# Three attention heads' bias bands added by TensorE in three 16-bit parts instead of two 32-bit parts

## The chip, the cores and the metric

The kernel runs on one core of a Trainium2 chip. The metric is the device time of one execution in microseconds (us); before, the median of three runs is 2453.97 us (2453.03 to 2454.3). One more execution was taken with the hardware profiler; all rows below come from it.

## What is computed

The program is a chain of six residual layers over x, four sequences of 1024 rows with 256 features: a mixture of experts, an attention, the mixture again, a quantized linear layer, a second attention of 16 heads, and the linear layer again. The change lies in the second attention:

```python
q = proj(Wq) / math.sqrt(DH)      # DH = 16, 16 heads
k = proj(Wk)
v = proj(Wv)
scores = jnp.einsum('bhid,bhjd->bhij', q, k)
i = jnp.arange(T)
dist = jnp.clip(i[:, None] - i[None, :], 0, MAX_REL)   # MAX_REL = 128
bias = rel[:, dist]
scores = scores + bias[None]
causal = i[:, None] >= i[None, :]
scores = jnp.where(causal[None, None], scores, -jnp.inf)
attn = jax.nn.softmax(scores, axis=-1)
y = jnp.einsum('bhij,bhjd->bhid', attn, v)
```

The bias of a head depends on the distance alone and is the same beyond 128, so after the far value is taken off it is zero everywhere but in a band of 256 columns beside the diagonal. The causal mask is put into the same band.

## The kernel before, in words

Two stages matter. The linear layer in front of the second attention (`linear`) carries other work in its gaps, step by step. `HeadTables` splits the attention's weights and builds the bands; `HeadProjection` normalizes, transposes and projects the first sequence. `beside_steps` sets their order: 28 steps of the tables come first, then each step of the projection, and beside every second one a further step of the tables. Each engine runs its own part of this list in order.

The tables are built for eight pairs of heads (`hp`). SP fetches a pair's band from a scratch tensor, TensorE (PE) flips it, ScalarE (ACT) copies it to `full` (L1672), and PE transposes it for the maxima (`flip_turn`). In step `part 0` ACT copies `full` into the first part of `band` (L1680), rounded to the 32-bit matmul format, and for every second pair one head's band to `band_dve` (L1679). In step `part 1` GpSimd (POOL) subtracts the first part from `full` and writes the second part (L1659), and ACT copies the transposed band to `band_q`. A pair's copy to `full` waits for the POOL subtraction of the pair before. POOL's queue also holds the gathers of the linear layer's input (L1379), whose sums VectorE (DVE) makes.

The heads' stage (`attention_heads`) then works on 16 units, each four heads (`HG`) of one sequence. A unit has 12 cells of key block (128 keys) and half of the queries (up to 512), and each cell has four scores, one for each head. PE multiplies a score (L2273) into one of three banks. In nine of the 12 cells the band meets the cell. There PE adds the band for the first three heads (`HP`): two matmuls of a 32-bit identity `ident_r` by the parts of `band` (L2277), with 256 columns in six cells and 128 in three. For the fourth head DVE adds `band_dve` in the bank (L2208). ACT takes the exponential (L2133), and PE multiplies it by the values (L2294). PE may start score n+1 only when the exponential of score n-2 is done.

Between the scores PE, in an order written out by `heads_order`, computes the scores of later units a first time (L2253) into three other banks. DVE takes their row maxima (L2170, L2179 and, with `band_q` added, L2182). In the first two units of a sequence the projection of the next one stands in the same lists.

## Time and profile before

| | before |
|---|---|
| median of the runs | 2453.97 us |
| the profiled execution | 2455.88 us |
| its span in the trace | 2453.8 us |
| PE busy | 2067.1 us (84%) |
| DVE busy | 1482.1 us (60%) |
| ACT busy | 955.9 us (39%) |
| POOL busy | 308.8 us (13%) |

The time of the profiled execution is its span and some 2 us around it. Matmuls overlap, and their ends are modelled: a matmul's duration is longer than its distance from the next one, so costs of PE are read from start to start. The chain of waits is followed back from the last instruction and says which engine's work set the end of the program; busy shares alone do not.

### The profile page before, as it was taken

What the parts mean: (1) busy time and instruction counts of PE and PEld (TensorE: products, weight loads), DVE (VectorE), ACT (ScalarE), POOL (GpSimd) and SP (SyncE); (2) the same over time, 40 slices, a digit from 0 to 9 for tenths busy, and PEclk for the clock granted to TensorE, in tenths of its full rate; (3) what the DMA queues carried; (4) which work ended last, traced back from release to release, by engine and by line L of the source; (5) the groups of instructions that cost most, each with busy time, mean ns of one, the idle gap of its engine ahead of it and who ended that gap; (6) DMA issues with size and microseconds to landing.
All of it is one profiled execution on the core that took longest, in us unless ns stands there. A gap on an engine that the chain in (4) does not pass through costs nothing.

```text
span 2453.8 us, 38491 instructions
## 1 busy us (share of the span) xinstructions
PE 2067.1 (84%) x12810; PEld 1556.0 (63%) x12810; DVE 1482.1 (60%) x4378; ACT 955.9 (39%) x1944; POOL 308.8 (13%) x300
## 2 busy tenths in 40 slices
PE   5689999966999975899999836578998998999966
PEld 3578888855878854788888725424554455545445
DVE  7844444446555578444444388677786686687548
ACT  4222232322333343223233234325555555655643
POOL 4420000022000033300000062311001101100000
PEclk8799999987999987999999967769999999999988
DMA  8111010111000022201010130342242242333002
GB/s 270 54 58 30 27 31 27 32 52 41 1 1 1 1 69 79 84 21 32 27 31 27 33 112 15 77 54 60 41 53 53 54 53 47 59 43 39 3 9 69
DMA packets 84043, 114.83 MB, mean 47 GB/s; under 512 B 12216, under 2 KB 73824, under 8 KB 80736
## 3 DMA queue, kind: packets, MB, share of 16 engines
q1 hardware_dynamic: 77424, 94.80, 17.5%
q0 software_dynamic: 6432, 17.57, 2.2%
q8 instruction: 113, 1.85, 0.3%
q14 instruction: 74, 0.61, 0.1%
HBM read 69.17 MB, written 43.17 MB: 46 GB/s over the span
## 4 chain that ended last, share of the span: by engine, by line
PE 61%; DVE 26%; ACT 4%; issue 4%; DMA 2%; POOL 2%; SPq 0%; DVEq 0%; ACTq 0%; POOLq 0%
PE psum L775 10%; PE psum L777 10%; PE psum L776 10%; PE psum L2294 4%; PE psum L126 4%; PE psum L128 4%; PE psum L127 4%; DVE mt L2182 4%; PE psum L2273 3%; PE psum L862 3%; DVE m L2170 3%; DVE m L2179 2%; PE psum L2253 2%; DVE stats L160 2%; PE psum L2277 2%
## 5 line engine op out<-in xcount | busy, mean ns | idle before, releaser
L2133 ACT ACTIVATE pt<-psum 128x512 f32<-128x512 f32 (+3 forms) x768 | 334.0, 492 | 273.0 <-DVE psum L2208 180.2
L740 DVE SCALAR_TENSOR_TENSOR h<-psum,xg,sg 128x128 f32<-128x128 f32 x592 | 166.6, 344 | 415.6 <-PE psum L862 415.6
L556 ACT ACTIVATE sg<-psum 128x512 f32<-128x512 f32 x180 | 107.7, 598 | 544.2 <-PE psum L777 544.2
L775 PE MATMUL psum<-w_hi,xt_hi 128*128 (+1 forms) x720 | 286.2, 398 | 17.9 <-DVE xt_lo L705 17.3
L776 PE MATMUL psum<-w_lo,xt_hi 128*128 (+1 forms) x720 | 284.2, 395 | 0.0
L777 PE MATMUL psum<-w_hi,xt_lo 128*128 (+1 forms) x720 | 283.7, 394 | 0.0
L2253 PE MATMUL psum<-ks,qs 96*128 96x512 bf16 (+3 forms) x768 | 234.8, 346 | 43.0 <-DMA ks<-qk_scr 18.8
L2273 PE MATMUL psum<-qs,ks 99*128 99x512 bf16 (+3 forms) x768 | 238.3, 333 | 24.7 <-ACT pt L2133 19.1
L775 PE MATMUL psum<-w_hi,ht_hi 128*128 (+1 forms) x720 | 217.1, 302 | 0.3
L2277 PE MATMUL psum<-band,ident_r 128*128 128x256 f32 (+1 forms) x864 | 215.0, 337 | 0.0
L2182 DVE CUSTOM_DVE_ANT_0 mt<-psum,band_q 128x256 bf16<-128x256 f32 (+1 forms) x512 | 204.2, 399 | 17.1 <-PE psum L2253 6.9
L777 PE MATMUL psum<-w_hi,ht_lo 128*128 (+1 forms) x720 | 203.2, 282 | 0.0
L776 PE MATMUL psum<-w_lo,ht_hi 128*128 (+1 forms) x720 | 201.9, 280 | 0.0
L2273 PEld LDWEIGHTS psum<-qs,ks 99*128 99x128 bf16 x768 | 68.8, 98 | 188.4 <-ACT pt L2133 112.3
L2170 DVE TENSOR_REDUCE m<-psum 128x1 f32<-128x512 f32 (+1 forms) x256 | 166.9, 652 | 34.0 <-PE psum L2253 30.4
L775 PEld LDWEIGHTS psum<-w_hi,xt_hi 128*128 128x128 f32 x720 | 137.0, 190 | 43.4 <-issue 19.4
L2277 PEld LDWEIGHTS psum<-band,ident_r 128*128 128x128 f32 x864 | 149.9, 194 | 19.0 <-issue 0.3
L2294 PE MATMUL psum<-pt,v 128*17 128x512 f32 (+3 forms) x1536 | 161.6, 494 | 0.0
L777 PEld LDWEIGHTS psum<-w_hi,xt_lo 128*128 128x128 f32 x720 | 136.8, 190 | 30.0
L776 PEld LDWEIGHTS psum<-w_lo,xt_hi 128*128 128x128 f32 x720 | 137.2, 190 | 22.6
L2253 PEld LDWEIGHTS psum<-ks,qs 96*128 96x128 bf16 x768 | 68.9, 99 | 117.6 <-DVE m L2182 45.7
L776 PEld LDWEIGHTS psum<-w_lo,ht_hi 128*128 128x128 f32 x720 | 136.4, 189 | 0.0
(283 smaller groups left out, 4248.6 us busy)
## 6 DMA issues: line engine op xcount, KB each, us to landing
xg<-w_dram SPq DMA_DIRECT2D x54, 256.0 KB, 3.2
qk_scr<-parts SPq DMA_DIRECT2D x32, 384.0 KB, 2.5
qs<-qk_scr SPq DMA_DIRECT2D x96, 128.0 KB, 7.0
ks<-qk_scr SPq DMA_DIRECT2D x96, 128.0 KB, 7.7
xg<-rows_in SPq DMA_DIRECT2D x74, 132.0 KB, 2.1
rows_out<-yb SPq DMA_DIRECT2D x74, 128.0 KB, 1.7
x<-x_dram SPq DMA_DIRECT2D x4, 1024.0 KB, 8.7
out_dram<-x SPq DMA_DIRECT2D x4, 1024.0 KB, 4.5
```

Of the source, the lines that this page charges most:

```text
L556: act.activation(sg[i % 2][:, :, :], up_banks(i)[:, :, 0:F], ACT.Silu).then_inc(*silu.up())
L740: ins = dve.scalar_tensor_tensor(out=h[i % 2][:, e, :], in0=u[:, e, :], scalar=xg[j % XSLOT][:, at:at + 1], in1=sg[i % 2][:, e, :], op0=AL ...
L775: pe.matmul(out, a[0], b[0], start=first, stop=False)
L776: pe.matmul(out, a[0], b[1], start=False, stop=False)
L777: return pe.matmul(out, a[1], b[0], start=False, stop=last)
L2133: act.activation(pt[n % NPT][:, 0:q1 - q0], st_bank(n)[:, 0:q1 - q0], ACT.Exp).then_inc(*exped.up())
L2170: dve.tensor_reduce(m3[u % 2][:, h * BT + t, 0:1], mx_ring.bank((kind, i))[:, 0:cut], AXIS.X, ALU.max).then_inc(*far_max.up())
L2182: dve.tensor_tensor_reduce(junk[:, 0:bw], bank[:, far - cut:w - cut], band_q[:, u % NHG * HG + h, 2 * P - bw:2 * P], 1.0, LOWEST, ALU.add, ...
L2253: pe.matmul(bank[:, 0:c1 - c0], qs[r][0:KS_ROWS, h, t * P:(t + 1) * P], ks[r][0:KS_ROWS, h, c0:c1], start=True, stop=True).then_inc(*(far_ ...
L2273: ins = pe.matmul(bank[:, 0:q1 - q0], ks[r][:, h, j * P:(j + 1) * P], qs[r][:, h, q0:q1], start=True, stop=not by_pe)
L2277: ins = pe.matmul(bank[:, 0:b1 - q0], tables.ident_r[:, :], band[:, part, u % NHG, h, q0 - j * P:b1 - j * P], start=False, stop=(part == 1))
L2294: ins = pe.matmul(y_banks[c][h * MQ:h * MQ + DH + 1, q0 - c * BANK:BANK], v1[b % 2][:, j, g * HG + h, :], slot[:, 0:(c + 1) * BANK - q0], ...
```

## The change

The bands of the three heads that PE adds are kept in three 16-bit parts instead of two 32-bit ones, and the identity that they are multiplied by is 16-bit too. So a band is three matmuls on PE instead of two. DVE adds the fourth head's band as before; the rewritten index and wait of that addition come to the same for one such head.

To make three parts, ACT writes the first part in 16 bits, POOL subtracts it from `full` into a new buffer `rest`, ACT writes the second part from `rest`, and POOL subtracts that from `rest` into the third part. This adds a step `part 2` for each pair, eight steps in all. The next pair's copy to `full` now waits for POOL's first subtraction (`rest_ok`), and POOL's first subtraction waits for the second one of the pair before (`left_ok`).

```diff
+        BPARTS = 3
...
-                self.ident_r = sb(stack, "ident_r", [P, P], F32R)
-                self.band = sb(stack, "band", [P, 2, NHG, HP, 2 * P], F32R)
-                self.band_dve = sb(stack, "band_dve", [P, NHG, 2 * P])
+                self.ident_b = sb(stack, "ident_b", [P, P], BF16)
+                self.band = sb(stack, "band", [P, BPARTS, NHG, HP, 2 * P], BF16)
+                self.band_dve = sb(stack, "band_dve", [P, NHG, HG - HP, 2 * P])
...
                     yield [("part", (hp, 1))]
+                    yield [("part", (hp, 2))]
...
-                elif kind == "part" and i[1] == 1:
+                elif kind == "part" and i[1] > 0:
                     hp, part = i
                     g, h0, n = self.heads_of(hp)
-                    pool.wait_ge(*self.part_ok(hp + 1))
-                    pool.tensor_tensor(self.band[:, 1, g, h0:h0 + n, :], self.full[:, 0:n, :],
-                                       self.band[:, 0, g, h0:h0 + n, :].bitcast(F32),
-                                       ALU.subtract).then_inc(*self.left_ok.up())
+                    near = lambda m: self.band[:, m, g, h0:h0 + n, :]
+                    if part == 1:
+                        if hp:
+                            pool.wait_ge(*self.left_ok(hp))
+                        pool.wait_ge(*self.part_ok(hp + 1))
+                        pool.tensor_tensor(self.rest[:, 0:n, :], self.full[:, 0:n, :], near(0),
+                                           ALU.subtract).then_inc(*self.rest_ok.up())
+                    else:
+                        pool.wait_ge(*self.mid_ok(hp + 1))
+                        pool.tensor_tensor(near(2), self.rest[:, 0:n, :], near(1),
+                                           ALU.subtract).then_inc(*self.left_ok.up())
...
                     if i:
-                        act.wait_ge(*self.left_ok(i))
+                        act.wait_ge(*self.rest_ok(i))
...
+                    if part == 2:
+                        act.wait_ge(*self.rest_ok(hp + 1))
+                        act.activation(self.band[:, 1, g, h0:h0 + n, :], self.rest[:, 0:n, :],
+                                       ACT.Copy).then_inc(*self.mid_ok.up())
...
-                                for part in range(2):
-                                    ins = pe.matmul(bank[:, 0:b1 - q0], tables.ident_r[:, :],
+                                for part in range(BPARTS):
+                                    ins = pe.matmul(bank[:, 0:b1 - q0], tables.ident_b[:, :],
                                                     band[:, part, u % NHG, h, q0 - j * P:b1 - j * P],
-                                                    start=False, stop=(part == 1))
+                                                    start=False, stop=(part == BPARTS - 1))
```

On PE the first cell of the first unit stood as follows before (`qs`, `ks`: the stacked queries and keys; L2273 a score, L2277 its band, L2253 a score for the maxima):

```order
L2273 MATMUL psum<-qs_133,ks_134 128x512
L2253 MATMUL psum<-ks_182,qs_181 128x512 x2
L2273 MATMUL psum<-qs_133,ks_134 128x512
L2277 MATMUL psum<-band,ident_r 128x256 x2
L2253 MATMUL psum<-ks_182,qs_181 128x128
L2273 MATMUL psum<-qs_133,ks_134 128x512
L2277 MATMUL psum<-band,ident_r 128x256 x2
```

And there it stands so now (lines are some 15 further down: L2288 a score, L2292 its band, L2268 a score for the maxima):

```order
L2288 MATMUL psum<-qs_133,ks_134 128x512
L2268 MATMUL psum<-ks_183,qs_182 128x512 x2
L2288 MATMUL psum<-qs_133,ks_134 128x512
L2292 MATMUL psum<-band,ident_b 128x256 x3
L2268 MATMUL psum<-ks_183,qs_182 128x128
L2288 MATMUL psum<-qs_133,ks_134 128x512
L2292 MATMUL psum<-band,ident_b 128x256 x3
```

Each band has a third matmul, and nothing else moved here.

On ACT the second half of the first sequence's projection stood so before, in the linear stage (`xn` the normalized rows, `xt_hi` and `rest` their transposed parts, `parts` the projected queries and keys, L1419 the linear layer's own):

```order
L1808 ACTIVATE xn<-xn,rstd_10 128x256 x4
L1817 ACTIVATE xt_hi<-psum,gamma_beta 128x512
L1819 ACTIVATE rest_131<-psum,gamma_beta 128x512
L1817 ACTIVATE xt_hi<-psum,gamma_beta 128x512
L1819 ACTIVATE rest_132<-psum,gamma_beta 128x512
L1828 ACTIVATE parts<-psum 128x512
L1831 ACTIVATE parts<-rest_131 128x512
L1419 ACTIVATE xt_hi<-psum 128x512 x2
```

And so now, with the last pair's steps among them:

```order
L1683 ACTIVATE band_full<-psum 128x512
L1823 ACTIVATE xn<-xn,rstd_10 128x256 x4
L1832 ACTIVATE xt_hi<-psum,gamma_beta 128x512
L1834 ACTIVATE rest_131<-psum,gamma_beta 128x512
L1690 ACTIVATE band_dve<-band_full 128x256
L1691 ACTIVATE band<-band_full 128x256
L1832 ACTIVATE xt_hi<-psum,gamma_beta 128x512
L1834 ACTIVATE rest_132<-psum,gamma_beta 128x512
L1843 ACTIVATE parts<-psum 128x512
L1846 ACTIVATE parts<-rest_131 128x512
L1699 ACTIVATE band_q<-psum 128x512
L1419 ACTIVATE xt_hi<-psum 128x512 x2
```

The copies of the last pair, which came before the projection, now stand inside it.

On POOL the same stretch read so before (`x` the residual rows, `xt_lo` and `parts` the projection's remainders):

```order
L1786 TENSOR_TENSOR x<-x,xn 128x1024
L1790 TENSOR_TENSOR xt_lo<-rest_131,xt_hi 128x512
L1790 TENSOR_TENSOR xt_lo<-rest_132,xt_hi 128x512
L1795 TENSOR_TENSOR parts<-rest_131,parts 128x512
L1795 TENSOR_TENSOR parts<-rest_132,parts 128x512
L1795 TENSOR_TENSOR parts<-rest_131,parts 128x512
L1795 TENSOR_TENSOR parts<-rest_132,parts 128x512
```

And so now:

```order
L1667 TENSOR_TENSOR band_rest<-band_full,band 128x512
L1671 TENSOR_TENSOR band<-band_rest,band 128x512
L1801 TENSOR_TENSOR x<-x,xn 128x1024
L1805 TENSOR_TENSOR xt_lo<-rest_131,xt_hi 128x512
L1805 TENSOR_TENSOR xt_lo<-rest_132,xt_hi 128x512
L1810 TENSOR_TENSOR parts<-rest_131,parts 128x512
L1667 TENSOR_TENSOR band_rest<-band_full,band 128x256
L1810 TENSOR_TENSOR parts<-rest_132,parts 128x512
L1810 TENSOR_TENSOR parts<-rest_131,parts 128x512
L1671 TENSOR_TENSOR band<-band_rest,band 128x256
L1810 TENSOR_TENSOR parts<-rest_132,parts 128x512
```

The two subtractions of each of the last two pairs now stand ahead of the projection's second half and within it.

## Rows read from the trace of the kernel before

**Rows 1.** The page, its first part: busy time, share and instructions of each engine.
```profile
PE 2067.1 (84%) x12810; PEld 1556.0 (63%) x12810; DVE 1482.1 (60%) x4378; ACT 955.9 (39%) x1944; POOL 308.8 (13%) x300
```

**Rows 2.** Windows of the heads' stage: length, each engine's busy us, clock, DMA.
```profile
1740.00:1780.00 40.00, 38.50 (x276) 19.35 (x276) 33.66 (x130) 23.07 (x53) 0.18 (x1) 1.00 0.33 42
...
2300.00:2340.00 40.00, 36.39 (x268) 17.96 (x265) 9.83 (x34) 26.59 (x62) 0.00 (x0) 1.00 0.01 2
```

**Rows 3.** The chain of waits from 1631 to 2357 us, shares by line.
```profile
by line: PE psum L2294 14.7%; DVE mt L2182 10.8%; PE psum L2273 10.7%; DVE m L2170 7.9%; issue 7.0%; PE psum L2253 6.4%; DVE m L2179 5.8%; PE psum L2277 5.1%; PE psum L126 3.3%; DVE psum L2208 3.1%; ACT pt L2133 2.8%; PE psum L128 2.4%; PE 
```

**Rows 4.** Grouped instructions, 1631 to 2357 us: busy us, mean ns, idle us before.
```profile
L2277 PE MATMUL psum<-band,ident_r 128*128 128x256 f32 x576 | 150.7, 350 | 0.0
L2277 PEld LDWEIGHTS psum<-band,ident_r 128*128 128x128 f32 x864 | 149.9, 194 | 19.0 <-issue 0.3
...
L2273 PEld LDWEIGHTS psum<-qs,ks 99*128 99x128 bf16 x766 | 68.6, 98 | 182.4 <-ACT pt L2133 112.3 <-issue 50.0
L2277 PE MATMUL psum<-band,ident_r 128*128 128x128 f32 x288 | 64.4, 311 | 0.0
...
L2273 PE MATMUL psum<-qs,ks 99*128 99x256 bf16 x128 | 32.2, 280 | 11.9 <-ACT pt L2133 11.9
...
L2273 PE MATMUL psum<-qs,ks 99*128 99x128 bf16 x128 | 28.4, 226 | 0.5 <-ACT pt L2133 0.4
```

**Rows 5.** Time line of PE, bands of 256 columns: start us, us, engine, line.
```profile
1756.98 0.38 PE L2273 MATMUL psum<-qs,ks 99*128 99x512 bf16 x1
1757.01 0.58 PE L2277 MATMUL psum<-band,ident_r 128*128 128x256 f32 x2
1757.45 0.39 PE L2273 MATMUL psum<-qs,ks 99*128 99x512 bf16 x1
```

**Rows 6.** Time line of PE, 16-bit matmuls of 256 and 512 columns.
```profile
1908.73 0.28 PE L2253 MATMUL psum<-ks,qs 96*128 96x256 bf16 x1
1908.84 0.38 PE L2273 MATMUL psum<-qs,ks 99*128 99x512 bf16 x1
1909.06 0.57 PE L2253 MATMUL psum<-ks,qs 96*128 96x512 bf16 x2
```

**Rows 7.** Time line of PE, bands of 128 columns behind scores of 512 and 128.
```profile
1777.24 0.38 PE L2273 MATMUL psum<-qs,ks 99*128 99x512 bf16 x1
...
1777.64 0.45 PE L2253 MATMUL psum<-ks,qs 96*128 96x384 bf16 x2
...
1779.49 0.22 PE L2273 MATMUL psum<-qs,ks 99*128 99x128 bf16 x1
...
1779.78 0.23 PE L2253 MATMUL psum<-ks,qs 96*128 96x128 bf16 x1
```

**Rows 8.** Time line of PE, a 16-bit matmul of 128 columns.
```profile
1773.11 0.22 PE L2253 MATMUL psum<-ks,qs 96*128 96x128 bf16 x1
1773.17 0.27 PE L2273 MATMUL psum<-qs,ks 99*128 99x256 bf16 x1
```

**Rows 9.** The chain's first and last band: start us, us, what.
```profile
1666.07 0.23 PE psum L2277 x2
...
2353.06 0.23 PE psum L2277 x2
```

**Rows 10.** Waits from 1631 to 2357 us: us in total, times, longest us.
```profile
ACT pt L2133 <- DVE psum L2208: 180.2, 113, 37.1
...
PEld psum L2273 <- ACT pt L2133: 112.3, 178, 3.4
```

**Rows 11.** The making of `band` (duration ns min/median/max), and one wait of ACT.
```profile
L1680 ACT ACTIVATE band<-band_full x8: 399/507/633, 1433.9 to 1505.8; 128x512 fp32r<-128x512 f32 x4, 128x256 fp32r<-128x256 f32 x4
L1659 POOL TENSOR_TENSOR band<-band_full,band x8: 730/1274/1705, 1441.0 to 1513.7; 128x512 fp32r<-128x512 f32 x4, 128x256 fp32r<-128x256 f32 x4
...
1449.57 0.60 ACT L1672 ACTIVATE band_full<-psum 128x512 f32<-128x512 f32 x1 [3.80 <-POOL band L1659]
```

**Rows 12.** The projection: a piece of the chain, and POOL's time line.
```profile
1558.76 0.68 ACT rest L1819
...
1568.68 1.17 POOL L1795 TENSOR_TENSOR parts<-rest,parts 128x512 bf16<-128x512 f32 x1 [2.43 <-ACT parts L1831]
```

More of the change, by code:

```diff
@@ L1561, in __init__ @@
                 self.flipped, self.fulled, self.flip_turned = S("flipped"), S("full"), S("flip_turned")
-                self.part_ok, self.left_ok, self.band_q_ok = S("band_part"), S("band_left"), S("band_q")
+                self.part_ok, self.rest_ok, self.mid_ok, self.left_ok, self.band_q_ok = (S(x) for x in (
+                    "band_part", "band_rest", "band_mid", "band_left", "band_q"))
             def allocate(self, stack):
@@ L1568, in allocate @@
                 self.stage = [sb(stack, f"table_stage{i}", [P, KD * D]) for i in range(2)]
-                self.full = sb(stack, "band_full", [P, 2, 2 * P])
+                self.full, self.rest = (sb(stack, s, [P, 2, 2 * P]) for s in ("band_full", "band_rest"))
             def order(self):
@@ L1635, in on_pool @@
                 if kind == "setup":
-                    pool.tensor_copy(self.ident_r[:, :], ident[:, :])
+                    pool.tensor_copy(self.ident_b[:, :], ident[:, :])
                     pool.memset(line[:, :], MASKED).then_inc(*self.line0.up())
@@ L1678, in on_act @@
                         if n < 2:
-                            act.activation(self.band_dve[:, g, :], self.full[:, n, :], ACT.Copy)
+                            act.activation(self.band_dve[:, g, h0 + n - HP:h0 + 2 - HP, :], self.full[:, n:2, :], ACT.Copy)
                         act.activation(self.band[:, 0, g, h0:h0 + n, :], self.full[:, 0:n, :],
                                        ACT.Copy).then_inc(*self.part_ok.up())
+                    if part == 2:
+                        act.wait_ge(*self.rest_ok(hp + 1))
+                        act.activation(self.band[:, 1, g, h0:h0 + n, :], self.rest[:, 0:n, :],
+                                       ACT.Copy).then_inc(*self.mid_ok.up())
                     if part == 1:
@@ L2129, in on_act @@
                             if near_of[cell] and h >= HP:
-                                act.wait_ge(*biased(u * len(near_cells) + near_cells.index(cell) + 1))
+                                act.wait_ge(*biased((u * len(near_cells) + near_cells.index(cell)) * (HG - HP) + HG - h))
                             else:
```

2 lines of the change are left out of this document (1 added, 1 removed).

## Prediction, made before the changed kernel ran

> **What bounds the kernel now.** I read the page first, then the grouped instructions of the stage that the change touches, then its chain of waits, and last single matmuls on the time line, because a mean duration does not tell how far apart pipelined matmuls run. The page [rows 1] shows TensorE (PE) busy for 84% of the span. The heads' stage lies between 1631 and 2357 us. Its windows [rows 2] show PE busy for 38.5 of 40 us and VectorE (DVE) for 33.7 in the middle of the stage, and at its end PE for 36.4 and DVE only for 9.8. So PE and DVE are both nearly full, and neither has the stage alone. The chain of waits says the same: band matmuls (L2277) hold 5.1% of these 726 us, or 37 us, while DVE's maxima (L2182, L2170 and L2179) hold 24.5% [rows 3]. The reader is to see two things. PE is busy, but only part of what its band matmuls do lies on the path. And the matmuls' mean durations (350 and 311 ns, against 280 and 226 ns of the 16-bit ones of the same widths [rows 4]) are no price: they overlap.
>
> **What one band costs on PE before.** On the time line [rows 5] the score matmul at 1756.98 us (512 columns, then a band of 256 columns in two parts) is followed by the next score at 1757.45, after 0.47 us. A 16-bit matmul of 512 columns without a band takes 0.22 us from start to start (1908.84 to 1909.06 [rows 6]). So two 32-bit parts of 256 columns take 0.25 us, 0.125 each. For 128 columns there are two cases [rows 7]: behind a score of 512 columns it is 1777.24 to 1777.64, 0.40 less 0.22, so 0.18; behind one of 128 columns it is 1779.49 to 1779.78, 0.29 less the score's own 0.06, so 0.23.
>
> **What one band will cost.** A 16-bit part is a matmul of the same kind as the score's. With 256 columns such a one takes 0.11 us from start to start (1908.73 to 1908.84 [rows 6]), and with 128 columns 0.06 (1773.11 to 1773.17 [rows 8]). The mean durations of the two widths differ by 54 ns [rows 4], the time of 128 columns; with that I take 0.109 and 0.057 inside the two roundings. Three parts are then 0.327 us for 256 columns and 0.171 for 128. The change gives TensorE half as many matmuls again, and a 16-bit one is hardly cheaper than a 32-bit one where 256 columns set the pace: +0.077 us. With 128 columns it saves 0.01 (behind 512) or 0.06 (behind 128).
> Counted over the stage: 576 matmuls of 256 columns are 288 bands, 288 of 128 columns are 144 [rows 4]; of these 48 stand behind a score of 512 columns (block 3 against the second query half) and 96 behind one of 128. That is 288 x 0.077 = +22.2 us, 48 x 0.01 and 96 x 0.06 = -6.2 us, in all **+16 us of TensorE's time**.
>
> The 16-bit identity must also be loaded more often, 1296 times instead of 864. A load lasts 194 ns for the 32-bit identity and 98 ns for 16-bit weights [rows 4], but the spacing of 0.06 us at 1773.11 [rows 8] holds for a matmul whose successor loaded weights of its own, so a 16-bit load fits under 128 columns. I put the loads at nothing; their cover is the matmul ahead. The Trainium skill, page "TensorE: Matmul & The Clock Gate", section "LDWEIGHTS (loading the stationary operand)", speaks against this: it gives a load the columns divided by 1.2 in ns, an estimated 107 ns for 128 columns, by which three parts of 128 columns would take 0.32 us and TensorE's total would be about +37 us. The trace's 0.06 us disagrees with that.
>
> **How much of it lies on the path.** The lower end comes from the chain: a path that exists can only become as long as its pieces. Between its first band piece (1666.07 us) and its last (2353.06) the chain holds 123 bands of 256 columns, 0.23 to 0.24 us each, and 39 of 128, 20 of them near 0.17 and 19 near 0.23 [rows 9]. Priced as above, 123 x 0.077 - 20 x 0.01 - 19 x 0.06 = +8 us. The upper end is the whole +16: PE sets the pace throughout. PE idles 112.3 us in 178 waits for ScalarE's exponentials before a score, and ScalarE idles 180.2 us for the sums that DVE makes of the fourth head [rows 10]; such waits swallow part of a later PE. I take **+10**, near the chain's end, since the windows show DVE close behind PE in the middle of the stage; only at its end, where DVE is busy for 9.8 of 40 us [rows 2], is PE alone. A chain read back from semaphores can also overstate PE, so the bound for a reading in which DVE paces is lower than +8: the share of L2277 in the chain, 37 us of the 103 us that bands take by the prices above, times +16 is +6, and I let it fall to +2.
>
> **Making the third part.** The tables' stage gains eight conversions on ScalarE (ACT) and eight subtractions on GpSimd (POOL), and its steps stretch by eight. The existing ones last 0.40 to 0.63 us on ACT and 0.73 to 1.71 us on POOL [rows 11]. Those of six pairs lie before about 1518 us, where the two engines have holes: ACT waited 3.8 us for the same POOL subtraction at 1449.57 [rows 11]. There the new waits (ACT's second part for POOL's remainder, POOL's third part for ACT) take the place of the wait on the old second part; POOL's gathers are queued behind, and DVE's combines wait for these, but the new wait is one of the old length. I take 0. The last pairs of heads (6 and 7) now fall into the projection, where the chain runs through ACT, POOL and PE in turn. There pair 7's two copies stand between the two halves of the turned input: the second half's last step (0.68 us at 1558.76) is on the chain [rows 12], and the copies ahead of it add about 0.3 + 0.4 us, below their 0.40 us each since ACT's instructions overlap. The rest of pairs 6 and 7 meets holes such as POOL's 2.43 us at 1568.68 [rows 12]. On SP the pairs' fetches stand ahead of the projection's stores as they did; that costs nothing. I take **+1** for this stage, 0 to +4; the upper end is that half of the eight subtractions, at 0.73 to 1.28, stand on the path.
>
> **Sum.** +10 +1 = +11 us. The profiled execution took 2455.88 us (2453.8 of span, 2.1 around it), so it would be 2466.9; the median of the runs stands 1.9 lower, at 2453.97, and gives **2465.0**. Some 0.2% (4.9 us) is what a measurement here can tell from no change.
>
> **Rivals.**
> 1. DVE paces the stage and PE's extra work falls into its waits. For it: the 24.5% of the chain in DVE's maxima [rows 3] and the 112.3 us of waits [rows 10]. Against it: PE at 38.5 of 40 us [rows 2]. It gives +2 to +4, about 2457.
> 2. PE paces the stage throughout. For it: the same 38.5 of 40 us. Against it: the DVE pieces of the chain. All of +16 plus 1 to 4 gives 2471 to 2474.
> 3. Faster: the loads of the 32-bit identity, not columns, space the bands everywhere. Then two loads of 194 ns give way to three of 98 [rows 4], -0.094 us for each of 432 bands, -41 us, of which the chain's share (37 of 103) is -15: 2439. It decides if a band of 256 columns costs as much as its two loads, 0.39 us; it costs 0.25 [rows 5].
> 4. The 16-bit loads do not hide behind each other when three stand in a row. Then a 128-column band costs 3 x 0.098 = 0.294: 48 x 0.114 + 96 x 0.064 = +11.6 instead of -6.2, +34 in all; at 10/16 on the path, +21 and +1: 2476. Against it: the 0.06 at 1773.11 [rows 8]. The Trainium skill's rule on loads, named above, is this rival's.
> 5. The third part comes at a price of its own: the projection's chain takes up each of the new steps of pairs 6 and 7, +4, beside the +10: 2468. Nothing in PE's prices changes; this is inside the range.
>
> **How the numbers follow.** Forecast (+6 to +14, the fifth with it) 0.56, the first 0.18, the second 0.16, the third 0.04, the fourth 0.06. The first lies mostly within 4.9 us; a little of the forecast may too. So faster 0.04, same 0.18, slower 0.78. The range runs from +2 (2456) to the second's upper end (2473), which leaves out the third, the fourth and the edge of the first.
>
> **What would show it.** In the profile after, the band matmuls' line has 1296 matmuls, with loads near 98 ns; in the time line a score of 512 columns with a band of 256 is 0.54 to 0.55 us from the next, and one of 128 columns 0.39; the chain's share of the band line grows from 5.1% to about 7%; the heads' stage is about 10 us longer, and its start moves by about 1 us. The forecast is wrong if three parts of 256 columns take 0.25 us or less, if the stage's length stays as it is while PE's waits for ACT (112.3 us [rows 10]) shrink by what the bands gained, or if the start of the heads moves by several us.

## The result, and the profile after

The changed kernel is slower. Timed beside the kernel before, its median was 2467.03 us against 2456.49, 10.5 us more; the ratio is 1.0037 with a 95% interval of [1.0023, 1.0052], or +9.1 us. In a second set it was 2463.22 against 2455.48, 7.7 us more; the ratio is 1.0032 [1.0019, 1.0044], or +7.9 us. The prediction was +11 us, 2465.0 on the base of 2453.97, with a range of +2 to +19. The total held, but two of its terms were wrong in opposite directions.

The profiled execution after took 2462.59 us, 6.7 more than the one before (2455.88). Cut at three instructions that stand in both kernels (POOL's copy of the identity, the first score and the band of the last score), the two spans compare so:

| us | before | after | difference |
|---|---|---|---|
| start to the tables' first step | 1409.60 | 1409.56 | 0.0 |
| tables and projection, to the first score | 220.42 | 223.52 | +3.1 |
| heads' stage, first to last score | 723.04 | 729.40 | +6.4 |
| after the last score | 100.76 | 98.32 | -2.4 |

The last line is no effect of the change: over the 14 profiles of this study this stretch took 98.1 to 100.8 us, in no order that follows what was edited. So two stretches hold the price: +6.4 where +10 was predicted, and +3.1 where +1 was.

First the page after, the line that answers to [rows 1]. PE has 432 matmuls more and is hardly busier by this line, PEld is less busy, and POOL has its eight subtractions:

```profile
PE 2071.6 (84%) x13242; PEld 1528.2 (62%) x13242; DVE 1486.7 (60%) x4378; ACT 964.0 (39%) x1952; POOL 317.3 (13%) x308
```

The grouped instructions of the heads' stage after, which answer to [rows 4] (busy us, mean ns, idle us before; L2292 is the band's line now):

```profile
L2292 PE MATMUL psum<-band,ident_b 128*128 128x256 bf16 x864 | 141.6, 273 | 0.0
...
L2292 PEld LDWEIGHTS psum<-band,ident_b 128*128 128x128 bf16 x1293 | 117.1, 98 | 45.8 <-issue 1.6
...
L2292 PE MATMUL psum<-band,ident_b 128*128 128x128 bf16 x429 | 46.8, 219 | 0.0
```

By busy time a band has become cheaper (141.6 + 46.8 us against 150.7 + 64.4), which is the trap of these columns: matmuls overlap. The time line of PE shows the price, from start to start (L2288 a score, L2268 a score for the maxima):

```profile
1760.56 0.38 PE L2288 MATMUL psum<-qs,ks 99*128 99x512 bf16 x1
1760.77 0.49 PE L2292 MATMUL psum<-band,ident_b 128*128 128x256 bf16 x3
1761.10 0.38 PE L2288 MATMUL psum<-qs,ks 99*128 99x512 bf16 x1
...
1781.11 0.38 PE L2288 MATMUL psum<-qs,ks 99*128 99x512 bf16 x1
1781.33 0.33 PE L2292 MATMUL psum<-band,ident_b 128*128 128x128 bf16 x3
1781.50 0.44 PE L2268 MATMUL psum<-ks,qs 96*128 96x384 bf16 x2
...
1783.36 0.22 PE L2288 MATMUL psum<-qs,ks 99*128 99x128 bf16 x1
1783.42 0.33 PE L2292 MATMUL psum<-band,ident_b 128*128 128x128 bf16 x3
1783.59 0.22 PE L2268 MATMUL psum<-ks,qs 96*128 96x128 bf16 x1
```

A score of 512 columns and its band of 256 now take 0.54 us instead of 0.47 [rows 5]; the medians over such cells from the third unit on are 0.547 and 0.467. A score of 512 with a band of 128 takes 0.39 instead of 0.40, and one of 128 with its band 0.23 instead of 0.29 [rows 7]. These are the prediction's prices to the hundredth. With the rounded 0.07 for a band of 256 instead of 0.077, the prediction's +16 us of PE's work becomes +14 (288 x 0.07 - 6.2); the expectations of the experiments below speak of that.

The chain of waits over the heads' stage after, by line, answers to [rows 3]. The band's share went from 5.1% to 8.1%, and the share of DVE's maxima (L2197, L2185, L2194) from 24.5% to 17.6%: PE has taken over part of a path that the two engines share.

```profile
by line: PE psum L2309 15.2%; PE psum L2288 12.2%; PE psum L2268 8.8%; PE psum L2292 8.1%; DVE mt L2197 7.7%; issue 6.3%; DVE m L2185 5.4%; DVE m L2194 4.5%; PE psum L126 3.3%; ACT pt L2148 3.1%; DVE psum L2223 2.9%; PE psum L2337 2.3%; PE 
```

**The stage cut into its 16 units.** The +6.4 us becomes plain when windows run from one unit's first score to the next one's. Four units before, as windows (length, busy us of PE, PEld, DVE, ACT and POOL, then PE's granted clock and last two figures of DMA): the sixth, ninth and tenth, which carry the projection of a later sequence, and the twelfth, which does not.

```profile
1880.18:1937.20 57.02, 51.50 (x340) 30.11 (x336) 38.18 (x128) 32.76 (x72) 10.93 (x10) 0.97 0.34 67
...
2011.72:2072.83 61.11, 53.24 (x339) 30.91 (x335) 41.32 (x145) 31.61 (x67) 8.47 (x7) 1.00 0.27 46
2072.83:2128.56 55.73, 50.14 (x339) 29.04 (x335) 38.20 (x129) 32.76 (x72) 10.93 (x10) 1.00 0.36 70
...
2165.68:2202.84 37.16, 35.71 (x260) 18.22 (x256) 30.45 (x117) 21.76 (x50) 0.18 (x1) 1.00 0.36 45
```

The same units after:

```profile
1884.77:1941.03 56.26, 50.98 (x367) 27.80 (x363) 38.35 (x129) 33.01 (x72) 10.92 (x10) 1.00 0.34 68
...
2016.76:2077.97 61.21, 54.20 (x366) 29.58 (x363) 41.21 (x144) 31.96 (x67) 8.48 (x7) 1.00 0.26 45
2077.97:2134.23 56.26, 50.98 (x367) 27.80 (x363) 38.36 (x129) 33.08 (x72) 10.92 (x10) 1.00 0.34 67
...
2172.03:2209.83 37.80, 36.77 (x287) 17.03 (x283) 30.46 (x117) 22.23 (x50) 0.18 (x1) 1.00 0.33 43
```

The twelfth unit grew by 0.64 us, and the seven units like it (third, fourth, seventh, eighth, eleventh, twelfth and fourteenth; "plain" below) by 0.62 on average, all of them at full clock. By the prediction's prices PE has 1.0 us more to do in each unit (+16 us over 16). The tenth, with the projection, grew by 0.53, and the ninth by 0.10 only. The sixth seems to have become shorter, from 57.02 to 56.26. Its clock column tells why: PE was granted 0.97 there before, on average between its two levels of 1.2 and 2.4 GHz, and 1.00 after. The dip lies between 1910 and 1920 us (0.83 there); from 1900 to 1910 us PE was busy for 8.36 us, just as in the same place of its twin, the tenth, which kept 1.00. The twin took 55.73 us, so the clock cost the kernel before 1.3 us in the sixth unit. With that unit at full clock the stage would have grown by 6.4 + 1.3 = 7.7 us, just under the +8 that the prediction read from the chain as the floor. The first unit was at 0.94 in both and is no measure: it took 62.33 us before and 62.03 after, and 62.3 in the two other profiles of kernels with three parts that are named further down (after_again and one_step).

The last two units are the prediction's "only at its end ... is PE alone". They grew hardly more than the plain ones, by 0.65 and 0.67 us, although DVE has little to do in them. The sixteenth, before and after:

```profile
2322.86:2353.06 30.20, 27.22 (x202) 13.71 (x198) 4.85 (x13) 20.82 (x49) 0.00 (x0) 1.00 0.00 1
```
```profile
2331.61:2362.48 30.87, 28.54 (x229) 12.41 (x225) 4.86 (x13) 20.93 (x49) 0.00 (x0) 1.00 0.01 1
```

What took up the rest there is shown by the runs without the fourth head's addition, below.

**Where the tables' +3.1 us arise.** The chain of waits in the first sequence's projection before (start us, us, what: L185 normalizes, L1871 turns the rows, L1790 and L1828 make the parts):

```profile
1547.14 1.29 DVE xn L185 x4
...
1556.09 0.45 PE psum L1871 x4
...
1559.51 1.27 POOL xt_lo L1790
...
1562.95 0.61 ACT parts L1828
```

And after:

```profile
1547.51 2.14 DVE xn L185 x4
...
1557.04 0.45 PE psum L1886 x4
...
1558.93 0.41 ACT band_dve L1690
1559.34 0.30 ACT band L1691
...
1561.06 1.26 POOL xt_lo L1805
```

The time lines of POOL and ACT after add two rows, and the line of the normalization gives its durations (ns, min/median/max):

```profile
1547.22 1.30 POOL L1671 TENSOR_TENSOR band<-band_rest,band 128x512 bf16<-128x512 f32 x1 [3.32 <-ACT band L1695]
```
```profile
1565.46 0.60 ACT L1843 ACTIVATE parts<-psum 128x512 bf16<-128x512 f32 x1 [4.48 <-PE psum L128]
```
```profile
L185 DVE TENSOR_SCALAR xn<-x,mean_var,rstd x4: 398/400/1249, 1547.4 to 1549.2; 128x256 f32<-128x256 f32 x4
```

Four pieces follow one another. The stretch starts 0.37 us later (1547.14 to 1547.51). DVE's normalization takes 2.14 us instead of 1.29, because one of its four instructions lasted 1249 ns instead of some 400: they began at 1547.4, while POOL was at the third part of pair 6 (1547.22 to 1548.52). The two copies of pair 7 stand on the chain with 0.41 + 0.30 us, as the prediction had them, and the start of L1805 is 1.55 us late by then. Last, PE's part of the projection up to ACT's L1843 takes 4.40 us (1561.06 to 1565.46) instead of 3.44, at a granted clock of 0.50, the lower level of 1.2 GHz throughout, against 0.78 in the windows of these matmuls (1562.45 to 1565.50 after, 1560.91 to 1562.95 before). Together that is +2.5 us at 1565.46, and +3.1 at the first score; the last 0.6 us were not taken apart.

This sum of pieces is one profile's, and the stretch is not the same length in every profile of the same tables. With the maxima as they are it took 220.4 and 220.6 us in two profiles with the tables of before, and 222.8 to 224.9 in five with the changed ones. The last piece, 4.40 us at 0.50, also came in the kernel with no third part at all (two_parts), whose whole stretch took 221.2 us. So that piece need not be the third part's.

### The profile page after: what moved, and what is told of

Its sections match the earlier page's. It is cut to its first block, busy times and chain, and to the rows that moved or that the text cites. A ratio compares the mean times of both kernels' runs of the same rounds, so it can differ in the third digit from the quotient of the medians.

```text
span 2460.8 us, 39378 instructions
## 1 busy us (share of the span) xinstructions
PE 2071.6 (84%) x13242; PEld 1528.2 (62%) x13242; DVE 1486.7 (60%) x4378; ACT 964.0 (39%) x1952; POOL 317.3 (13%) x308
## 3 DMA queue, kind: packets, MB, share of 16 engines
q1 hardware_dynamic: 77424, 94.80, 17.6%
## 4 chain that ended last, share of the span: by engine, by line
PE 63%; DVE 24%; ACT 4%; issue 4%; DMA 2%; POOL 2%; SPq 0%; DVEq 0%; ACTq 0%; POOLq 0%
PE psum L775 10%; PE psum L777 10%; PE psum L776 10%; PE psum L2309 5%; PE psum L126 4%; PE psum L2288 4%; PE psum L128 4%; PE psum L127 4%; PE psum L862 3%; DVE mt L2197 3%; PE psum L2268 3%; PE psum L2292 2%; DVE stats L160 2%; DVE m L2185 2%; DVE m L2194 2%
## 5 line engine op out<-in xcount | busy, mean ns | idle before, releaser
L2148 ACT ACTIVATE pt<-psum 128x512 f32<-128x512 f32 (+3 forms) x768 | 339.0, 492 | 276.4 <-DVE psum L2223 180.1
L2268 PE MATMUL psum<-ks,qs 96*128 96x512 bf16 (+3 forms) x768 | 232.1, 342 | 40.3 <-DMA ks<-qk_scr 19.1
L2288 PE MATMUL psum<-qs,ks 99*128 99x512 bf16 (+3 forms) x768 | 237.7, 333 | 21.9 <-ACT pt L2148 14.5
L2197 DVE CUSTOM_DVE_ANT_0 mt<-psum,band_q 128x256 bf16<-128x256 f32 (+1 forms) x512 | 204.7, 400 | 17.0 <-PE psum L2268 6.7
L2185 DVE TENSOR_REDUCE m<-psum 128x1 f32<-128x512 f32 (+1 forms) x256 | 167.1, 653 | 37.5 <-PE psum L2268 33.6
L2292 PE MATMUL psum<-band,ident_b 128*128 128x256 bf16 (+1 forms) x1296 | 188.7, 255 | 0.0
L2288 PEld LDWEIGHTS psum<-qs,ks 99*128 99x128 bf16 x768 | 68.6, 97 | 187.3 <-ACT pt L2148 120.6
L2292 PEld LDWEIGHTS psum<-band,ident_b 128*128 128x128 bf16 x1296 | 117.3, 98 | 45.8 <-issue 1.6
L2268 PEld LDWEIGHTS psum<-ks,qs 96*128 96x128 bf16 x768 | 73.6, 98 | 114.5 <-DVE m L2197 47.9
```

The source lines that it names most:

```text
L2148: act.activation(pt[n % NPT][:, 0:q1 - q0], st_bank(n)[:, 0:q1 - q0], ACT.Exp).then_inc(*exped.up())
L2185: dve.tensor_reduce(m3[u % 2][:, h * BT + t, 0:1], mx_ring.bank((kind, i))[:, 0:cut], AXIS.X, ALU.max).then_inc(*far_max.up())
L2197: dve.tensor_tensor_reduce(junk[:, 0:bw], bank[:, far - cut:w - cut], band_q[:, u % NHG * HG + h, 2 * P - bw:2 * P], 1.0, LOWEST, ALU.add, ...
L2268: pe.matmul(bank[:, 0:c1 - c0], qs[r][0:KS_ROWS, h, t * P:(t + 1) * P], ks[r][0:KS_ROWS, h, c0:c1], start=True, stop=True).then_inc(*(far_ ...
L2288: ins = pe.matmul(bank[:, 0:q1 - q0], ks[r][:, h, j * P:(j + 1) * P], qs[r][:, h, q0:q1], start=True, stop=not by_pe)
L2292: ins = pe.matmul(bank[:, 0:b1 - q0], tables.ident_b[:, :], band[:, part, u % NHG, h, q0 - j * P:b1 - j * P], start=False, stop=(part == B ...
```

## The experiments

All times stand beside runs of the kernel before on the same chip, and every ratio is to those.

### Fewer matmuls, the tables as they are

In no_third_matmul the third matmul of each band is left out, and the third part is made but not used.

```diff
-                                for part in range(BPARTS):
+                                for part in range(BPARTS - 1):
...
-                                                    start=False, stop=(part == BPARTS - 1))
+                                                    start=False, stop=(part == BPARTS - 2))
```

> The changed kernel, with the tables made in three 16-bit parts, but TensorE adds only the first two (the third part, the smallest remainder, is left out of the scores). Theory (columns set TensorE's price, and about half of it lies on the path): a band of 256 columns takes 2 x 0.109 = 0.218 us instead of 0.25 before, one of 128 columns 0.114 instead of 0.18 to 0.23, together -24 us of TensorE's time against before; half of it on the path is -12, and the tables' +3 remain: -9 us, ratio 0.9963. Against the changed kernel that is 39.6 us of TensorE's time for the third matmuls. Rival (VectorE paces the stage, TensorE's time falls into its waits): 0 to -3 and the tables' +3, ratio 1.000. Rival (the price of the change is in the tables and not in the third matmul): ratio as the changed kernel's, 1.0037.

Measured: 2454.2 us, 0.9992 [0.9982, 1.0002], so the rival's number. With 39.5 us of PE's work gone (288 x 0.109 + 144 x 0.056) the time fell by 11 us from the changed kernel and only just to the kernel before. A plain unit took 37.09 us, against 37.35 before and 37.97 after. What PE saves below the kernel before goes for the most part into waits (0.26 us of a plain unit is seen, of some 1.5 that the expectation's -24 us give each of the 16 units); of what it gets beyond it, 0.62 of 1.0 is seen.

### Two 16-bit parts throughout

In two_parts no third part is made or multiplied, and the steps stand as before; POOL's one subtraction writes the second part straight into `band`, and its wait for the pair before is gone.

```diff
-        BPARTS = 3
+        BPARTS = 2
...
-                    yield [("part", (hp, 2))]
...
-                        if hp:
-                            pool.wait_ge(*self.left_ok(hp))
...
-                        pool.tensor_tensor(self.rest[:, 0:n, :], self.full[:, 0:n, :], near(0),
+                        pool.tensor_tensor(near(1), self.full[:, 0:n, :], near(0),
```

> Two 16-bit parts all through: the tables make two (the third part is left out), in the order of steps of the kernel before, and TensorE adds two. Theory: -24 us of TensorE's time, half of it on the path, and no price in the tables: -12 us, ratio 0.995, and the first score starts where it did before (1630 us after the span's start, within 0.5). Rival (VectorE paces): 0 to -3, ratio 0.999. If the start of the scores stays at +3 us as in the changed kernel, the tables' price does not come from the third part's steps.

Measured: 2450.37 us, 0.9981 [0.9972, 0.999], 4.1 us below the kernel before by the medians. The theory's -12 us did not come, and the rival's 0 to -3 is nearer. The first score came at 1630.7 us. The stage took 717.2 us and its plain unit 37.09, as in the experiment above. The twelfth unit, as a window:

```profile
2161.85:2198.75 36.90, 35.11 (x259) 14.46 (x256) 30.40 (x117) 21.52 (x50) 0.18 (x1) 1.00 0.36 45
```

The unit is 0.26 us shorter than the twelfth before, and DVE's 30.4 us have not moved. This kernel and the one above also give the price of the third part in the tables alone: tables and projection took 221.2 us here and 224.6 with the third part made, +3.4 from one profile each, and the times lie 3.8 us apart by the medians and 2.7 by the ratios.

### The two subtractions in one step

In one_step the third part gets no step of its own; the tables' steps do not stretch, and pair 7's copies stand where they did.

```diff
-                    yield [("part", (hp, 1))]
-                    yield [("part", (hp, 2))]
+                    yield [("part", (hp, 1)), ("part", (hp, 2))]
```

> The changed kernel, with the third part made in the same step as the second, so that the tables have as many steps as before and the last pairs' work does not move into the projection. Theory (the +3 us ahead of the first score come from where the steps stand): the first score starts within 0.5 us of before's 1630.0, and the kernel is some 2.5 us faster than the changed one, ratio 1.0027. Rival (the price is the eight conversions and eight subtractions themselves, wherever they stand): the first score stays at about 1633, ratio 1.0037. Rival (waits in the shorter order now hold up VectorE's part of the stage): later than 1633.

Measured: 2463.08 us, 1.0034 [1.0023, 1.0045], and 224.6 us for tables and projection. The two causes named above were indeed gone: no copies stood between the halves, and the normalization took its old time,

```profile
1548.43 1.30 DVE xn L185 x4
```

but counted from POOL's copy of the identity (1407.21 here) it began at 141.2 us instead of 137.5, 3.7 us later. Of these, 1.7 us arose in the tables' own part, up to PE's first transpose of the projection (108.1 to 109.8 us). A further 1.1 us is the clock's: PE's part of the projection's first half took 2.94 us at 0.50, the level of 1.2 GHz, instead of 1.80 at 0.87. Here, and before:

```profile
1526.76:1529.70 2.94, 2.94 (x7) 2.36 (x8) 0.00 (x0) 0.00 (x1) 0.00 (x0) 0.50 0.00 0
```
```profile
1526.57:1528.37 1.80, 1.80 (x7) 1.48 (x8) 0.00 (x0) 0.01 (x1) 0.00 (x0) 0.87 0.00 0
```

The tables need not be the cause of the rest either. One profile with the tables and steps of before (before_short_no_add, further down, whose edit touches nothing ahead of this place) also reached the normalization at 141.1 us, with 109.3 us for the tables' own part and 2.94 us at 0.52 for PE's. From the normalization to the first score one_step took 83.4 us, against 82.9 before and 85.6 after. So behind the normalization the steps' place does make most of the price, as the theory had it; ahead of it this run cannot tell. Nor can its time: the interval holds the theory's 1.0027 as well as the rival's 1.0037.

### A fourth matmul

In fourth_matmul the third part is added twice; the output then has it twice.

```diff
-                                for part in range(BPARTS):
+                                for n_th, part in enumerate((0, 1, 2, 2)):
...
-                                                    start=False, stop=(part == BPARTS - 1))
+                                                    start=False, stop=(n_th == 3))
```

> The changed kernel with a fourth matmul for each band, which adds the third part a second time (so the smallest remainder is counted twice). Theory: 288 x 0.109 + 144 x 0.057 = +39.6 us of TensorE's time more than the changed kernel; TensorE now holds more of the path, 0.6 to 0.8 of it: +24 to +32, ratio 1.0135 to 1.0165. Rival (about four tenths of what TensorE gains or loses is on the path, however much it is): +16, ratio 1.010. Rival (VectorE paces): +4, ratio 1.005.

Measured: 2484.55 us, 1.0117 [1.0102, 1.0133]. Over the changed kernel (1.0037) that is +19.7 us for 39.5 us of PE's work, a half, where the third matmul cost 11 us over no_third_matmul, somewhat over a quarter. A plain unit took 39.27 us, +1.30 for 2.47 us of PE's work. So there is no single share: the longer PE works, the more of it is seen. The size was between theory and rival.

### The fourth head's addition left out

DVE's addition of the fourth head's band, and ACT's wait for it, are taken out of three kernels: with two 16-bit parts (two_no_add), with two 32-bit parts (before_no_add) and with three 16-bit parts (after_no_add).

```diff
-                            if near_of[cell] and h >= HP:
+                            if False:
...
-                            if near_of[i[1]] and h >= HP:
+                            if False:
```

> Left out of this kernel: the fourth head's band altogether (DVE's 144 additions at L2208, 55.5 us, and ACT's wait for them), and the third part of the other three heads. It is the low point of a row of three, beside before_no_add (two 32-bit parts) and after_no_add (three 16-bit parts). Theory (PE and DVE take the path in turn; DVE's addition stands in both engines' way since ACT's exponential, and so PE's score after the next, waits for it): without it PE holds more of the path, so the time falls by 10 to 35 us below two_parts, and the kernels of the row stand apart by more than with the addition: after_no_add is 14 to 18 us above two_no_add in the stage of the heads per 35 to 40 us of TensorE's time saved, against 12 us with it (729.4 against 717.2). Rival (the addition is hidden, PE's waits come from DVE's maxima and PE's own order): the time is within 5 us of two_parts and the distances stay as they are, 12 us in the stage.

> Left out: the fourth head's band altogether; otherwise the kernel before. Theory (the addition is one of the things that PE waits for): 2425 to 2445 us. Rival (hidden): 2450 to 2454 us. Beside after_no_add it gives the price of the change without the addition.

> Left out: the fourth head's band altogether; otherwise the changed kernel. Theory (PE and DVE in turn, with DVE's part now shorter): it stands 12 to 17 us above before_no_add (0.0050 to 0.0070 of the time), against 9 us (0.0037) with the addition, because a larger part of TensorE's extra 14 us now lies on the path. Rival (the part of the extra that waits take up has nothing to do with the addition): 8 to 10 us above before_no_add, as with it.

Measured: 2422.86 us (0.9878 [0.9863, 0.9893]), 2432.1 us (0.9905 [0.989, 0.9921]) and 2440.37 us (0.9945 [0.9932, 0.9959]). The addition is far from hidden: without it 22 to 28 us are gone, as the theories had it. But the distance between before and after, 8.3 us by the medians and 0.0040 by the ratios, was the rival's, and the stage grew by 5.4 us only. The units tell why the stage is no measure here. The fifth, sixth and tenth unit without the addition, two 32-bit parts first:

```profile
1814.31:1876.58 62.27, 55.84 (x339) 31.68 (x336) 38.58 (x136) 32.73 (x67) 8.48 (x7) 0.95 0.26 45
1876.58:1930.44 53.86, 49.97 (x340) 28.94 (x336) 35.77 (x120) 33.21 (x72) 10.93 (x10) 1.00 0.34 68
2063.06:2116.93 53.87, 49.97 (x340) 28.94 (x336) 35.78 (x120) 33.20 (x72) 10.94 (x10) 1.00 0.35 72
```

and three 16-bit parts:

```profile
1814.15:1874.16 60.01, 53.84 (x367) 29.67 (x363) 38.63 (x135) 32.71 (x67) 8.47 (x7) 1.00 0.27 46
1874.16:1928.62 54.46, 50.67 (x366) 27.92 (x363) 35.92 (x120) 33.21 (x72) 10.94 (x10) 1.00 0.34 68
2064.20:2118.64 54.44, 50.65 (x367) 27.91 (x363) 35.91 (x120) 33.28 (x72) 10.92 (x10) 1.00 0.35 70
```

The fifth unit shrank by 2.3 us although PE had more to do: its clock was 0.95 with two parts and 1.00 with three. At equal clock, in the sixth and tenth, it is +0.6 with the third part, and the plain units grew by 0.81 us (36.17 to 36.98), against 0.62 with the addition. In the units that can be compared, the theory's direction is right. Between two and three 16-bit parts it is right in size too: the stage grew by 16.9 us without the addition (14 to 18 expected) against 12.2 with it, and a plain unit by 1.28 against 0.88.

The sixteenth unit shows it best, since DVE makes no maxima there. Without the addition, two 32-bit parts and then three 16-bit ones:

```profile
2303.30:2330.82 27.52, 26.30 (x202) 13.69 (x198) 1.36 (x4) 21.07 (x49) 0.00 (x0) 1.00 0.01 1
```
```profile
2309.45:2338.33 28.88, 27.49 (x229) 12.82 (x225) 1.36 (x4) 21.79 (x49) 0.00 (x0) 1.00 0.01 1
```

It grew by 1.36 us, twice the 0.67 with the addition. Nine additions of 0.30 to 0.43 us each, with ACT's waits for them, took up half of PE's extra work in a unit where DVE is busy for 16% of the time.

### DVE's maxima shortened

In before_short_max and after_short_max the maxima of the keys beyond the band read 64 columns only, without and with the change. The maximum over the other columns is left out.

```diff
-                            dve.tensor_reduce(m3[u % 2][:, h * BT + t, 0:1], mx_ring.bank((kind, i))[:, 0:cut], AXIS.X,
+                            dve.tensor_reduce(m3[u % 2][:, h * BT + t, 0:1], mx_ring.bank((kind, i))[:, 0:min(64, cut)], AXIS.X,
...
-                                dve.tensor_reduce(m3[u % 2][:, h * BT + t, 1:2], bank[:, 0:far - cut], AXIS.X, ALU.max)
+                                dve.tensor_reduce(m3[u % 2][:, h * BT + t, 1:2], bank[:, 0:min(64, far - cut)], AXIS.X, ALU.max)
```

> The kernel before, but DVE's maxima of the keys beyond the band (L2170, 240 of 512 columns at 652 ns, and L2179, 240 of up to 256 at 350 ns) read the first 64 columns only; what is left out is the maximum over the other columns, and the banks come free earlier. DVE has some 150 us less to do in the stage of the heads, and all its additions of the fourth head's band stay. Both theories: clearly faster than before, by 20 to 60 us, since these maxima hold 14% of the chain [rows 3]. It serves as the base for after_short_max.

> The changed kernel with the same shortened maxima. Theory (DVE's maxima are what swallows half of TensorE's extra work): with DVE out of the way nearly all of the 14 us of TensorE's extra lies on the path, so the stage of the heads is 11 to 15 us longer than in before_short_max (6.4 with the full maxima), and the time 14 to 18 us above it (0.0055 to 0.0075). Rival (it is swallowed by TensorE's waits for ScalarE's exponentials, which stand in a fixed order and stay when the maxima go): the stage is 4 to 8 us longer, and the time 8 to 10 us above before_short_max (0.0033 to 0.0042).

Measured: 2407.13 us (0.98 [0.9787, 0.9814]) and 2420.12 us (0.9852 [0.9837, 0.9867]), 13.0 us apart, against 8 to 9 with the full maxima. The first is 49 us faster than the kernel before, inside the 20 to 60 expected. The stage grew by 9.1 us, between the theory's 11 to 15 and the rival's 4 to 8. In that sum the first unit shrank by 1.4 us, at a clock of 0.89 without the change and 0.93 with it. The plain units grew by 0.83 us (34.84 to 35.67), and the sixteenth, which has no maxima to shorten, by the same 0.67 as with all of them.

### Both lightened

Both edits above at once, the addition left out and the maxima shortened, without the change (before_short_no_add) and with it (after_short_no_add).

> The kernel before with both of DVE's parts lightened at once: the maxima of the keys beyond the band read 64 columns only, and the fourth head's band is left out altogether. It is the base for after_short_no_add. Expected: faster than each of the two alone (2407 and 2432 us).

> The changed kernel with both of DVE's parts lightened. Theory (DVE swallowed the rest, in the additions that the exponential waits for): nothing of DVE is left on TensorE's way, so all of TensorE's extra 14 us is seen: the stage of the heads is 12 to 15 us longer than in before_short_no_add (9.1 with the maxima alone lightened, 5.4 with the addition alone left out), and the time 14 to 18 us above it (0.0060 to 0.0076). Rival (the rest is swallowed by TensorE's waits for ScalarE's exponentials themselves): the stage stays 8 to 11 us longer, the time 10 to 13 us above.

Measured: 2388.16 us (0.9725 [0.9711, 0.9738]) and 2400.86 us (0.9784 [0.9771, 0.9797]), 12.7 us apart by the medians, which is the rival's figure, and 14.5 by the ratios (0.0059), just short of the theory's. The stage grew by 12.2 us, as the theory had it, and a plain unit by 0.92 us (34.27 to 35.18). The whole time is no clean measure of it: in this pair of profiles tables and projection took 1.5 us less with the change (218.6 to 217.1), because before_short_no_add reached the normalization so late. The chain of the twelfth unit, by line, with two 32-bit parts and with three 16-bit ones, has no DVE left in it:

```profile
by line: PE psum L2294 27.6%; PE psum L2273 26.3%; PE psum L2253 23.9%; PE psum L2277 18.0%; PE psum L2304 2.6%; ACT pt L2133 1.8%; issue 0.3%; ACTq L2132 0.0%
```
```profile
by line: PE psum L2309 26.9%; PE psum L2288 25.4%; PE psum L2268 22.4%; PE psum L2292 21.3%; PE psum L2319 2.5%; ACT pt L2148 1.7%; issue 0.3%; ACTq L2147 0.0%
```

The same unit in the two kernels of the case still has DVE on its chain, before 

```profile
by line: PE psum L2294 20.0%; DVE mt L2182 16.7%; PE psum L2273 13.6%; DVE m L2170 11.3%; PE psum L2253 9.1%; DVE m L2179 8.9%; issue 6.4%; PE psum L2277 6.2%; DVE psum L2208 3.1%; ACT pt L2133 2.7%; PE psum L2304 1.8%; DVE m L2182 0.5%; DV
```

and after:

```profile
by line: PE psum L2309 23.1%; PE psum L2288 18.2%; PE psum L2268 16.0%; PE psum L2292 14.0%; DVE mt L2197 8.2%; DVE m L2194 5.0%; DVE m L2185 4.5%; issue 3.8%; DVE psum L2223 2.6%; ACT pt L2148 2.6%; PE psum L2319 1.7%; DVE m L2197 0.3%; DV
```

So the row runs:

| DVE's work | plain unit, two 32-bit parts | three 16-bit parts | growth |
|---|---|---|---|
| all | 37.35 | 37.97 | 0.62 |
| without the addition | 36.17 | 36.98 | 0.81 |
| maxima shortened | 34.84 | 35.67 | 0.83 |
| neither | 34.27 | 35.18 | 0.92 |

The less DVE has to do, the more of PE's extra 1.0 us appears. That settles what swallowed most of the rest in the plain units: DVE's maxima and its addition, 0.2 us each when one of them is lightened and 0.3 together. In the sixteenth unit it is the addition alone.

### The changed kernel once more

> The changed kernel once more, unchanged, for a second profile beside a second set of timed runs: the first profiled execution (2462.59 us) was the shortest of its six (median 2467.03). Theory (the stage of the heads takes up about half of TensorE's extra 14 us): the stage is 728 to 732 us long (723.0 before, 729.4 in the first profile), and the first score stands at 1632 to 1634 us. Rival (the first profile flattered the stage, and the prediction's +10 was right): 732 to 735 us. The time is 8 to 11 us above before in both.

Measured (after_again): 2463.22 us, 1.0032 [1.0019, 1.0044]. The stage took 729.58 us and the first score stood at 1632.0; with one_step, whose heads' stage is the same (729.61), three profiles agree within 0.2 us. The first profile had not flattered the stage. The time, 7.7 us above before by the medians, lies just under the 8 to 11 expected.

## Why the prediction came out right, and which terms did not

**PE's prices: right.** Bands of 256 columns at +0.07 and of 128 at -0.01 and -0.06 stand in the time line as forecast, and with DVE out of the way a plain unit grew by 0.92 us of the 1.0 that the sum of +16 us gives it. Read from start to start there, in the twelfth unit, the growth of 0.96 us is +1.55 on the 18 bands of 256 columns, -0.40 on the nine of 128 and -0.19 on the matmuls that come next: behind a 32-bit band each of these took some 9 ns longer.

**Loads of the identity: right.** Three parts of 128 columns behind their score take 0.17 us (1783.42 to 1783.59), although each load lasts 98 ns: the fourth rival, with three loads in a row at 0.294 us, fell. The Trainium skill's figure for a load, named in the prediction, would give 0.32 us there if loads paced the matmuls; the measured 0.17 shows that they do not in this stream. The third rival, by which fewer 32-bit loads would make the kernel faster, fell with the +0.07 at 256 columns.

**The share that lies on the path: mis-sized, +10 where it was +6.4, or 7.7 at equal clock.** The step "I take +10, near the chain's end" moved up from the chain's floor of +8 because PE looked full at 38.5 of 40 us. The floor was the better reading. Raising it was wrong for a reason that the units show: that window [rows 2] says how full PE is, not what ends its unit, and in the twelfth unit DVE still held a fifth of the chain after the change. Nor was PE alone at the stage's end, as the 9.8 of 40 us of DVE led the prediction to say: the sixteenth unit grew by 0.67 us with DVE's additions and by 1.36 without them. That the profile fell as far below the floor as +6.4 is the clock's doing, 1.3 us in one unit of the kernel before. In the other direction the chain's pieces give no such bound: two_parts took some 1.5 us of PE's work out of a unit and won 0.26. That DVE's pieces then ended last is the likely reason.

**The tables: mis-sized, +1 where it was +3.1.** The measured +3.1 is inside the prediction's own 0 to +4. The copies between the halves cost what was said. Two things were not seen. "I take 0" for the steps moved past other work looked only at queues and waits; POOL's new subtraction of pair 6 then ran beside DVE's normalization and held one of its instructions for 0.85 us. The Trainium skill, page "SBUF — State Buffer", section "SBUF: two separate sides", tells of ports that DVE, in certain operations, and GpSimd hold in turn, the other being blocked for a whole instruction; the 1249 ns beside POOL's 1.30 us agree with that. Whether this normalization is one of these operations no run shows apart from the delay itself. And PE's stretch behind it met a lower clock, 0.50 instead of 0.78, +0.96 us, which no sum of durations shows and which two_parts met too. The fifth rival had the place right, a price in the projection, but gave another cause, the steps of pairs 6 and 7 on the chain one by one.

**The total: right by compensation.** +10 and +1 were forecast; 6.4 (7.7 at equal clock) and 3.1 came. That the two misses nearly cancel is luck. The range's upper end, 2473, is a microsecond below the 2474 that the second rival's sum gives. The first rival, that DVE paces and the change costs +2 to +4, fell with the plain units' 0.62 of 1.0; the second, that PE paces throughout, is what the kernels with a lighter DVE became.

What stays open: what ends the units with the projection. The ninth grew by 0.10 us and the tenth by 0.53 of the 1.0 that PE's prices give, and even with DVE lightened these were 0.32 and 0.67. The projection's own chain through ACT, POOL and DVE is a likely reason, but no run took it apart. Nor was it settled how much of the tables' +3.1 is the third part's and how much the clock's: one_step met a lower clock ahead of the normalization, and single profiles of the same tables differ by some 2 us.

## What to carry to other kernels

Price an edit of a shared stage unit by unit, between two instances of the same instruction, with the granted clock beside each unit: a total of a stage mixes units that take up all of the extra work with units that take none, and a single unit at 0.97 of the clock can hide a microsecond. When two engines hold a path in turn, as here, work added to one is seen in part and work taken from it is seen less: two 16-bit parts won some 5 us and three lost 8 to 9, with 39.5 us of TensorE's work between them. A low busy share does not put an engine out of the way: VectorE at 16% took up half of the extra work in the last unit. And before a subtraction is moved to GpSimd "into a hole", look at what VectorE does at that time, not only at GpSimd's queue.

## What was not expected of the hardware

- Beside a POOL subtraction of 128x512 that ran from 1547.22 for 1.30 us, one DVE normalization of 128x256 took 1249 ns instead of 400. All seven profiles with that subtraction beside it show one such instruction (1247 to 1254 ns), and the seven without show none (409 at most).
- A 32-bit identity's load lasts 194 ns and a 16-bit one's 98, and yet two 32-bit parts of 256 columns cost 0.24 to 0.25 us and three 16-bit ones 0.33: at 256 columns a matmul of either kind takes 0.11 to 0.125 us, and only at 128 columns is the 16-bit kind clearly cheaper, 0.057 us against 0.09 or more.
- The granted clock of PE in the heads' stage is not the same from profile to profile, nor from a unit to its twin: the sixth unit before took 57.02 us at 0.97 and its twin 55.73 at 1.00. With no third matmul, both of these units stood at 0.97 and took 56.51 us; with two parts, at 1.00, they took 55.43.
